# Rebuilding the input projections of an attention stage: two heads per transpose, keys first, rotation on GpSimd, the batch loop unrolled

## What is computed

```python
DIM, CTX_DIM, N_HEADS, HEAD_DIM = 512, 256, 32, 16
q = (layernorm(x) @ Wq).reshape(b, n, N_HEADS, HEAD_DIM)
k, v = jnp.split(ctx @ Wkv, 2, axis=-1)            # ctx: 4 x 512 x 256
q = apply_axial_rope(q, pos_map)                   # x1*cos - x2*sin, x1*sin + x2*cos
k = apply_axial_rope(k, ctx_pos_map)
w = jax.nn.softmax(jnp.einsum('bqhd,bkhd->bhqk', q, k) * scale, axis=-1)
x = x + jnp.einsum('bhqk,bkhd->bqhd', w, v).reshape(b, n, DIM) @ Wout + bout
```

## Time and profile before

| | |
|---|---|
| median of 3 runs | 1996.19 us (1995.73 to 1999.33) |
| profiled execution, its own time | 2000.66 us |
| its span, first to last instruction | 1998.9 us |
| mean granted TensorE clock | 0.90 |
| busy over the span: PE, DVE, ACT, POOL | 1572.8 us (79%), 1382.2 us (69%), 895.0 us (45%), 777.2 us (39%) |
| attention, from its setup to its last addition | about 769 to 1561 us of the span |

### The profile page before, as it was taken

How to read it: one execution, slowest core, us unless ns; L and a number is a source line. 1 busy time by engine, 2 the same in 40 slices (tenths; PEclk the granted TensorE clock), 3 DMA queues, 4 the chain that set the end, 5 groups by cost and what they waited for, 6 DMA issues and landing times. The chain is left out here.

```text
span 1998.9 us, 20908 instructions
## 1 busy us (share of the span) xinstructions
PE 1572.8 (79%) x6475; PEld 642.6 (32%) x6475; DVE 1382.2 (69%) x2071; ACT 895.0 (45%) x1157; POOL 777.2 (39%) x518
## 2 busy tenths in 40 slices
PE   6988989876506762899889988998898269898995
PEld 2333334322303321422342244224322123333332
DVE  6999999999663536588368747854784778455552
ACT  4765665643302001446535643663365244445542
POOL 4999999999153271300120022002100024233331
PEclk8998989988657995979999999999999679999998
DMA  6454555544773524000000000000000710000002
GB/s 220 139 151 143 150 147 141 149 138 136 154 171 104 106 85 164 1 1 1 11 1 1 2 12 1 1 1 12 1 1 1 158 45 1 0 1 0 0 0 84
DMA packets 65675, 131.83 MB, mean 66 GB/s; under 512 B 11536, under 2 KB 11792, under 8 KB 64800
## 3 DMA queue, kind: packets, MB, share of 16 engines
q1 hardware_dynamic: 49728, 95.81, 16.5%
q0 software_dynamic: 7168, 25.19, 5.7%
q10 hardware_dynamic: 8672, 9.50, 1.7%
HBM read 134.13 MB, written 12.87 MB: 74 GB/s over the span
## 5 line engine op out<-in xcount | busy, mean ns | idle before, releaser
L363 POOL TENSOR_TENSOR ssm_dBu<-ssm_du,ssm_BC 128x1024 f32<-128x1024 f32 x128 | 303.4, 2375 | 16.4 <-DVE ssm_du L399 16.4
L258 PE MATMUL ssm_psY<-ssm_hC,ident 128*128 128x512 f32 x512 | 255.8, 632 | 43.5 <-POOL ssm_hC L370 31.0
L1280 DVE TENSOR_REDUCE soft_next_mx<-soft_next_psS 128x1 f32<-128x512 f32 x384 | 248.2, 686 | 50.9 <-PE soft_next_psS L1168 48.4
L327 ACT ACTIVATE ssm_dA<-ssm_delta,ssm_negA 128x512 f32<-128x512 f32 x256 | 165.3, 682 | 170.0 <-DVE ssm_hC L419 168.6
L1326 ACT ACTIVATE soft_next_Pr<-soft_next_psT 128x1024 f32<-128x1024 f32 x192 | 188.9, 1019 | 114.3 <-PE soft_next_psT L1195 114.0
L1601 POOL TENSOR_TENSOR mlp_both<-mlp_first,mlp_third 128x512 f32<-128x512 f32 x88 | 125.1, 1422 | 283.1 <-DVE mlp_first L1543 143.7
L1081 POOL TENSOR_TENSOR att_QS<-att_rot,att_QS 128x1024 f16<-128x1024 f32 x16 | 34.1, 2128 | 509.7 <-ACT att_QS L1070 509.7
L1543 DVE SCALAR_TENSOR_TENSOR mlp_first<-mlp_psQ,mlp_s_gu,mlp_first 128x512 f32<-128x512 f32 x176 | 131.8, 749 | 127.7 <-ACT mlp_first L1579 117.7
L464 DVE TENSOR_TENSOR_SCAN ssm_dA<-ssm_dA,ssm_dBu 128x512 f32<-128x512 f32 x144 | 174.1, 1219 | 20.6 <-ACT ssm_dA L327 14.1
L1628 PE MATMUL mlp_psD<-mlp_Wd,mlp_hT 128*128 128x512 f32 x352 | 170.6, 629 | 10.3 <-DVE mlp_hT L1524 10.3
L1613 PE MATMUL mlp_psQ<-mlp_xh,mlp_Vgu 128*128 128x512 f16 x352 | 135.8, 386 | 49.9 <-PEq L64 40.1
(11 more groups left out here) (292 smaller groups left out, 2516.6 us busy)
## 6 DMA issues: line engine op xcount, KB each, us to landing
ssm_BC<-bc_rows SPq DMA_DIRECT2D x128, 512.0 KB, 4.8
moe_W<-in_masksT POOLq DMA_DIRECT2D x32, 512.0 KB, 9.2
deq_words<-in_gate_upT SPq DMA_DIRECT2D x32, 176.0 KB, 14.3
moe_XP<-sorted_rows ACTq DMA_DIRECT2D x4, 1030.0 KB, 22.3
X<-in_x SPq DMA_DIRECT2D x4, 1024.0 KB, 10.7
moe_XP<-results SPq DMA_DIRECT2D x4, 1024.0 KB, 9.1
out_x<-X SPq DMA_DIRECT2D x1, 4096.0 KB, 12.5
mlp_Wd<-in_downT ACTq DMA_DIRECT2D x8, 352.0 KB, 20.5
```

The lines of the kernel that those rows point to most:

```text
L258: nc.tensor.matmul(psY[:, w, :], ident[:], hC[:, w, g % RC, :], start=False, stop=(n == DS - 1)).then_inc(summed, 1)
L327: nc.scalar.activation(dA[:, q % RA, :], delta[:, b % 2, e, :], ACT.Exp, scale=negA[:, e, n:n + 1]).then_inc(dA_done, 1)
L363: nc.gpsimd.tensor_tensor(dBu[:, g % RB], du[:, b % 2, hh * W:(hh + 1) * W, :], BC[:, g % RING, 0, :].unsqueeze(1).broadcast_to([P, W, S]) ...
L1280: nc.vector.tensor_reduce(mx[:, m % 3, qt, j:j + 1], psS[:, i % 2, :], AX.X, ALU.max).then_inc(maxed, 1)
```

## The change

In words, for `stage_attention` alone:

- Setup: the contexts of all four batches are loaded here (batch 0 ahead of the weights, and waited for; 1 to 3 behind the bias, waited for by SP in the first project_in). The statistics are those of batch 0's 4 tiles alone. DVE's two memsets of the operand buffers go. POOL's memset of V is smaller (559 instead of 1024 columns a tile), and POOL sets rows 64 and 65 of KT (16384 f16 elements each) to one.
- project_in: the order is keys 0, keys 1, queries 0, keys 2, queries 1, keys 3, queries 2, queries 3. PE begins with keys and values and turns the rows between. `rot`, `t_cos`, `t_sin` and the operand buffer are doubled. DVE makes the two products only; POOL adds and subtracts (two operations of 128 x 256), for operand k+1 ahead of the low part of operand k. A head has 64 columns, and one transpose turns two heads (16 for each operand and tile); ACT copies partitions 0 to 63 of every fill, DVE 64 to 127.
- attend: scores contract over 64 partitions, transposed scores over 66; V's heads lie 17 columns apart. In the first attend DVE makes the statistics of the 12 other tiles: two `bn_stats` behind the 13th maximum of groups 0 to 5, 12 `bn_aggr` in group 6, root and reciprocal at the end. Four more semaphores.
- The hardware loop over batches 1 to 3 is written out.

```diff
+        parts16 = sb("parts16", [P, 2, H, HW], F16)
+        rot = sb("rot", [P, 2, D])
...
+                    sp.dma_start(ctxT[:, 0], ins["ctxT"][0].rearrange("(c p) s -> p c s", p=P)).then_inc(ctx_in[0], 16)
...
+                    for k in range(1, B):
+                        sp.dma_start(ctxT[:, k], ins["ctxT"][k].rearrange("(c p) s -> p c s", p=P)).then_inc(ctx_in[k], 16)
                     sp.wait_ge(loaded, 64)
+                    sp.wait_ge(ctx_in[0], 16)
...
+                    nc.gpsimd.memset(KT[HW:HK], 1.0).then_inc(consts, 1)
...
-                    layernorm_stats(nc, dve, chain, [X[:, t, :] for t in range(TILES)], stats, mv)
+                    layernorm_stats(nc, dve, chain, [X[:, t, :] for t in range(NT)], stats, mv)
...
+            ORDER = ((KEYS, 0), (KEYS, 1), (0, 0), (KEYS, 2), (0, 1), (KEYS, 3), (0, 2), (0, 3))
+            FILLS = 2
...
+                        def project(k):
+                            s, t = ORDER[k]
+                            if k >= 2:
+                                pe.wait_ge(taken, k - 1)
...
+                        def turn_parts(k):
+                            pe.wait_ge(hi_done, k + 1)
+                            pe.wait_ge(lo_done, k + 1)
+                            for f in range(FILLS):
+                                i = FILLS * k + f
+                                if i >= 3:
+                                    pe.wait_ge(evac_a, i - 2)
+                                    pe.wait_ge(evac_v, i - 2)
+                                for h in range(8):
+                                    mm = nc.tensor.transpose(psP[:, i % 3, h, :], parts16[:, k % 2, 2 * (8 * f + h):2 * (8 * f + h) + 2, :], ident16[:])
+                                mm.then_inc(parts, 1)
+
+                        project(0)
+                        project(1)
+                        project_values(0)
+                        turn_rows(0)
+                        turn_rows(1)
+                        project_values(1)
+                        turn_rows(2)
+                        turn_rows(3)
+                        for k in range(len(ORDER)):
+                            if k + 2 < len(ORDER):
+                                project(k + 2)
+                            if 1 <= k < NT - 1:
+                                project_values(k + 1)
+                            turn_parts(k)
...
+                        keep_turned(0)
+                        keep_values(0)
+                        high_parts(0)
+                        for t in range(1, NT):
+                            keep_turned(t)
+                        for k in range(len(ORDER)):
+                            if k + 1 < len(ORDER):
+                                high_parts(k + 1)
+                            if k < NT - 1:
+                                keep_values(k + 1)
+                            keep_first(k)
...
+                        def rotate(k):
+                            pool.wait_ge(cos_done, k + 1)
+                            pool.wait_ge(taken, k + 1)
+                            if k >= 2:
+                                pool.wait_ge(hi_done, k - 1)
+                                pool.wait_ge(lo_done, k - 1)
+                            c2, s2, r2 = (x[:, k % 2, :].rearrange("p (a w) -> p a w", w=2) for x in (t_cos, t_sin, rot))
+                            nc.gpsimd.tensor_tensor(r2[:, :, 0], c2[:, :, 0], s2[:, :, 1], ALU.subtract).then_inc(own, 1)
+                            nc.gpsimd.tensor_tensor(r2[:, :, 1], s2[:, :, 0], c2[:, :, 1], ALU.add).then_inc(rot_done, 1)
...
+                        rotate(0)
+                        for k in range(len(ORDER)):
+                            if k + 1 < len(ORDER):
+                                rotate(k + 1)
+                            low_parts(k)
...
+                        for k in range(len(ORDER)):
+                            take(k)
+                            if k >= 2:
+                                keep_second(k - 2)
+                        keep_second(len(ORDER) - 2)
+                        keep_second(len(ORDER) - 1)
...
-                            nc.tensor.matmul(psS[:, i % 2, :], QT[:, g * G + j, qt * P:(qt + 1) * P], KT[:, g * G + j, :],
+                            nc.tensor.matmul(psS[:, i % 2, :], QT[0:HW, g * G + j, qt * P:(qt + 1) * P], KT[0:HW, g * G + j, :],
...
+                        def row_stats(g):
+                            if 0 <= g < 6:
+                                for t in (NT + 2 * g, NT + 2 * g + 1):
+                                    rest.mark(nc.vector.bn_stats(stats[:, t, :], X[:, t, :]))
...
+                                if first and n == 12:
+                                    row_stats(g)
...
-        with nc.Fori(1, B) as b:
-            project_in(b, "next")
-            attend(b, b - 1, "next")
+        for b in range(1, B):
+            project_in(b, f"next{b}")
+            attend(b, b - 1, f"next{b}")
```

More of the change, by code:

```diff
@@ L950, in _ @@
                     act.wait_ge(mv_done, 1)
[L951 removed]
+                    nc.scalar.activation(rstd[:, 0:NT], mv[:, 0:NT, 1:2], ACT.Sqrt).then_inc(rooted, 1)
                 @block.vector
@@ L957, in _ @@
                         chain.mark(nc.vector.memset(freq[:].rearrange("p (a f) -> p a f", f=HALF)[:, :, j:j + 1], 10000.0 ** (-j / HALF)))
-                    chain.mark(nc.vector.memset(QS[0][:, :, HW:], 0.0))
-                    chain.link(nc.vector.memset(QS[1][:, :, HW:], 0.0))
-                    chain.mark(nc.vector.memset(QS[1][:, :, HW:HW + 2], 1.0))
+                    chain.wait()
                     dve.wait_ge(pos_in, 16)
@@ L974, in _ @@
                     dve.wait_ge(rooted, 1)
-                    chain.mark(nc.vector.reciprocal(rstd[:], rstd[:]))
+                    chain.mark(nc.vector.reciprocal(rstd[:, 0:NT], rstd[:, 0:NT]))
             c_.clear()
@@ new lines, in keep_first @@
+                        def keep_first(k):
+                            for f in range(FILLS):
+                                i = FILLS * k + f
+                                act.wait_ge(parts, i + 1)
+                                nc.scalar.activation(kept(k, f, 0), psP[0:HW, i % 3], ACT.Copy).then_inc(evac_a, 1)
+                        keep_turned(0)
[3 more added lines that the diff above has]
+                            keep_turned(t)
@@ L1084, in _, with take @@
                     @block.vector
                     def _(dve):
-                        chain = Tally(dve, own)
+                        def take(k):
+                            s, t = ORDER[k]
+                            dve.wait_ge(proj, k + 1)
+                            if k >= 2:
+                                dve.wait_ge(rot_done, k - 1)
+                            src = psQ[:, k % 2, :].rearrange("p (h a w) -> p h a w", h=H, w=2)
+                            cos, sin = (table4[:, s, w, b, t, :].unsqueeze(1).unsqueeze(3).broadcast_to([P, H, FQ, 2]) for w in range(2))
+                            nc.vector.tensor_tensor(t_cos[:, k % 2, :].rearrange("p (h a w) -> p h a w", h=H, w=2), src, cos, ALU.mult).then_inc(cos_done, 1)
+                            nc.vector.tensor_tensor(t_sin[:, k % 2, :].rearrange("p (h a w) -> p h a w", h=H, w=2), src, sin, ALU.mult).then_inc(taken, 1)
@@ L1129, in attend @@
                 turned, xT_done, proj, biased, added = (s_.sem(n) for n in ("turned", "xT_done", "proj", "biased", "added"))
+                first = run == "first"
+                stat_own, var_done, var_rooted, rstd_done = (s_.sem(n) for n in ("stat_own", "var_done", "var_rooted", "rstd_done"))
                 LAG = 2
@@ L1328, in _ @@
                                     send_maxima(g + LAG - 1)
+                            if first and g == NG - 1:
+                                act.wait_ge(var_done, 1)
+                                nc.scalar.activation(rstd[:, NT:], mv[:, NT:, 1:2], ACT.Sqrt).then_inc(var_rooted, 1)
                     @block.gpsimd
```

167 lines of the change are left out of this document (73 added, 94 removed).

## The result

The changed kernel takes **2125.86 us** (median of 4 runs, 2117.95 to 2126.71) against 1997.76 of the kernel before beside it (1995.73 to 1999.67): ratio 1.0633, 95% interval 1.0604 to 1.0661. 1972.7 was forecast, and the range ended at 1988. The profiled execution has a span of 2124.9 us, 126.0 more than before.

A forecast was written before the change was run, and what follows sets the result against it. PE, nearly full, and the chain between engines were taken to bound project_in. Terms -27.3 - 4.0 + 3.5 + 0.25 + 2.5 + 1.6 = -23.5 us took 1996.2 to 1972.7 us; range 1963 to 1988.

The forecast's parts named there:

- The step that failed: Attends: score matmuls over 64 or 66 of 128 partitions cost nothing, if the clock stays.
- The rival that named it: Attends: half-filled array keeps PE's clock low; groups over 22 us, +270 us, 2240 in all; chance 0.05.
- The setup: Setup: nothing booked; DVE's shorter statistics give no gain, as POOL's KT memset of 13.7 us ends at 785.0.
- project_in: Each batch's project_in: 50.0 us from less PE work and a shorter chain; 6.8 us saved, 27.3 over four.
- the rival of 1.2: project_in: POOL's rotations slow, 1.2 us each; sum -8, time 1988; chance 0.14.
- The layout: project_in step by step, from DVE's first instruction to ACT's last copy: ends at 49.3 us.
- the 0.7 added: project_in: the old order, laid out alike, ended 0.7 us below measured; added to give 50.0.
- The bound of 0.6: project_in: POOL's rotation operation of 256 elements, lower bound about 0.55 to 0.6 us; 0.6 taken.
- The statistics: First attend: DVE's added statistics cost 0.6 us in each of six groups, 3.5 lost; final reciprocal 0.25.
- The loop: Borders between batches: writing out the loop saves 2.0 us twice, 4.0 in all.
- Cold starts and semaphores: Three attends starting at low clock: 0.8 us each, 2.5 lost; 32 more semaphores cleared over the stage: 1.6 lost.

The follow-up runs named there:

- Experiments 1: Kernel before, fewer rows contracted: scores 64 2048.46 us; transposed scores 66 2003.71; both 66 2071.66; both 96 2000.99.
- experiment 2: Changed kernel, both score matmuls over 128 rows, rows 64 to 127 zeroed by DVE in the setup: 1976.29 us; scores alone so: 1978.89.
- experiment 3: Changed kernel with POOL's KT memset waiting for DVE's angles: 2094.23 us; then all 128 rows contracted, no POOL memset of KT, ones by DMA: 1973.35.
- Experiment 5: Rotation back on DVE, against the changed kernel with 128 rows contracted and no POOL memset of KT (1973.35 us): 1956.99 us.
- experiment 4: Statistics of all 16 tiles back in the setup, against the changed kernel with 128 rows and no POOL memset of KT (1973.35 us): 1971.58 us.
- experiment 6: Kernel before with only the hardware loop over batches 1 to 3 written out: 1988.12 us, ratio 0.9936.

## Why the prediction was wrong

- **The step that failed** is "Matmuls over 64 or 66 of 128 partitions stream the same 512 columns: nothing, if the clock stays". It cost about 150 us. The columns are the same; but the clock didn't stay: it came back 97 us later in the first attend, and in the others it fell again behind the projecting out, for 24, 72 and 72 us. And there is a second price that the sentence did not foresee, the open weight loads, which last for every warm group. Experiments 1 and 2 show both.
- The rival that named it had the right mechanism and sign, and a chance of 0.05. Its condition was met ten times over (38 us an attend where 3 would decide), its price was not: I had the whole attend cold, 22 us a group and +270. Cold are two to five groups of an attend, at up to 25 us, the first ones in batch 0 and those behind the projecting out in the others, and it comes to +151 with the warm part. What I held against it, "with V's 32 columns the late groups stay at 1.00", compares columns with rows. And the earlier trace rows had the warning in it: the scores over all 128 rows were cold for 18 us with PE in use; I took the end of that stretch as given by PE's time in use, when the rows in use were about to be halved.
- **The setup** ("So I book nothing for the setup") cost 4.5. The length of POOL's memset was right (13.75 against 13.7) and so was its end relative to the setup. What I missed is that it holds DVE. I asked only which engine ends last, not what they share. The Trainium skill (SBUF — State Buffer, SBUF: two separate sides) has the rule: DVE and GpSimd share a port pair that one of them locks for a whole instruction; DVE needs it in its faster modes, among others. By experiment 3 the rows agree: a `tensor_scalar` is held 13.07 and 11.07 us, `bn_stats`, `bn_aggr` and a DVE memset (6.88 us, in the kernel of experiment 2) are not.
- **project_in**: 50.0 forecast, 50.1 measured in batch 1, 27.3 against 27.1 over four. That close a hit is luck. PE's head ran as laid out (queries 0 done at 16.0, not 15.9), but queries 3 were done at 40.1, not 39.1, and the last low part at 47.4, not 46.1; 0.4 of that is the rotation, which took 0.84 us, not 0.6 (the rival of 1.2 did not come). The layout ended at 49.3, and the 0.7 added because it had missed the old order by as much happened to cover the rest. The bound of 0.6 was read too low as well: 512 elements in 1.19 and 1024 in 2.13 lie on a line that gives 0.7 for 256. Experiment 5 shows that moving the rotation to POOL was a loss of 3.3 to 4.5 us a batch inside a net gain.
- **The statistics**: 0.44 us a group against 0.6. With all rows contracted the first attend is 3.0 us longer than before; 3.75 were forecast. Moving them gained nothing in the total (experiment 4).
- **The loop**: 3.0 and 4.3 us in experiment 6, 3.4 and 3.0 in the kernel of experiment 2, against 2.0 each.
- **Cold starts and semaphores**, 2.5 and 1.6: with all rows contracted the last attend took 131.9 against 131.8, so neither shows.
- With the rows and the setup as I took them, the sum would have come out lower than forecast, not higher: in the kernel of experiment 2 four project_in and four attends together are 31.3 us shorter than before.

## What to carry to other kernels

Before contracting over fewer partitions to save nothing but zeros, look for a stretch at 0.50 in the kernel before: if matmuls of that kind have to bring the clock back, or to hold it after other work, keep them over all 128 (or 96) partitions, and keep neighbours at the same rows. Give a long POOL instruction, even a memset, a place where DVE has no SBUF to SBUF work. And test the parts of a change alone: here one part took back about five times what project_in, statistics and loop gained together (150 against 31 us), and another lost inside a part that gained.

## What the runs showed of the hardware

- How soon TensorE leaves 1.2 GHz depends on the rows that its matmuls use, with PE in use without a gap: in the first attend part of one group is cold where the scores use 128 or 96, and one to five groups where they use 64 or 66. Rows of zeros count as used.
- The rows also decide whether it keeps 2.4 GHz. At 64 and 66 rows it fell back to 1.2 GHz in each of three attends after the projecting out (128 rows) had ended (1.00 in 1282 to 1308, 0.50 in 1310 to 1380, PE in use for 70.00 of 70 us); with both at 128 or 96 it never did.
- How long such a stretch lasts isn't settled: batch 1's attend differs from its neighbours' (153.2 against 174.5), the kernel of experiment 3 had two cold groups in its first attend where the changed one had five, and the same matmuls that didn't bring the clock back for 70 us then ran at 1.00 to the end. No run here tells what decides it.
- Weight loads before a matmul over more than 64 rows lay open behind one over 64 (0.32 against 0.22 us from start to start), not between 66 and 128.
- An f16 memset on POOL costs 0.84 ns an element in each partition, about what fp32 does (0.86). A DVE `tensor_scalar` on 4 elements took 11 us beside it, and a DVE `tensor_tensor` of 0.42 us up to 1.80 beside a `tensor_tensor` on POOL.
